# A graph layer and a routed mixture of experts on one core: first weight loads, plan words and the order of the layer products

## The reference, cut to what matters

```python
def graph(x, adj, ...):                       # 4-bit activations, 3-bit weights
    x = act_quant(layernorm(x)); w = weight_quant((w - mean) / std)
    support = act_quant(relu(x @ w))
    return (adj / s) @ support * s
def ffn(x, ...):                              # top 2 of 16 experts
    logits = x @ Wr + br
    topk_w, topk_idx = top_k(softmax(logits), 2); topk_w /= sum(topk_w)
    h = gelu(layernorm(x @ W1[e] + b1[e]) * g1[e] + be1[e])
    y = h @ W2[e] + b2[e]                     # of the two chosen experts, weighted by topk_w
x = x + graph(layernorm(x), adj, ...)
x = x + ffn(layernorm(x))
```

## Time and profile before

| | us |
|---|---|
| median of 3 runs (562.1 to 565.27) | 562.18 |
| the profiled execution | 563.38 |
| its span, first to last instruction | 561.6 |
| PE busy | 499.5 (89%) |
| DVE busy | 352.4 (63%) |
| ACT busy | 290.8 (52%) |
| POOL busy | 234.3 (42%) |

### The profile page before, as it was taken

How to read it: one execution, slowest core, us unless ns; L and a number is a source line. 1 busy time by engine, 2 the same in 40 slices (tenths; PEclk the granted TensorE clock), 3 DMA queues, 4 the chain that set the end, 5 groups by cost and what they waited for, 6 DMA issues and landing times.

```text
span 561.6 us, 10545 instructions
## 1 busy us (share of the span) xinstructions
PE 499.5 (89%) x2384; PEld 405.3 (72%) x2385; DVE 352.4 (63%) x703; ACT 290.8 (52%) x488; POOL 234.3 (42%) x303
## 2 busy tenths in 40 slices
PE   1789999999999984788999999997997999999991
PEld 1568887788777763766887788886876888778881
DVE  5797855646667584477566667666766856666440
ACT  2664644434243413326567666765866766664440
POOL 5584502321625352244344444443434454444441
PEclk9999999999999995579999999997998999999996
DMA  8522215555444528138657776778498676534442
GB/s 303 198 76 75 84 50 193 198 168 188 130 174 152 187 77 312 41 125 286 164 126 194 187 203 154 180 195 216 123 299 213 158 218 152 146 60 78 77 81 46
DMA packets 33192, 88.29 MB, mean 157 GB/s; under 512 B 6064, under 2 KB 6208, under 8 KB 33040
## 3 DMA queue, kind: packets, MB, share of 16 engines
q1 hardware_dynamic: 18912, 56.53, 30.7%
q0 software_dynamic: 9648, 23.09, 20.9%
q10 hardware_dynamic: 4608, 8.39, 3.9%
HBM read 68.60 MB, written 19.40 MB: 157 GB/s over the span
## 4 chain that ended last, share of the span: by engine, by line
PE 51%; DVE 18%; ACT 8%; issue 7%; POOL 6%; DMA 4%; DVEq 2%; ACTq 1%; SPq 1%; POOLq 0%
PE ps L1407 10%; PE ps L1406 10%; PE ps L1408 10%; PE ps L1253 5%; PE ps L1240 4%; DVE w_lo L1172 3%; PE ps L1403 3%; PE ps L1426 3%; ACT w_hi L803 2%; POOL rstd L555 2%; DMA w_raw<-in_w 2%; DVE adj_lo L922 2%; ACT adj_hi L671 2%; PE ps L1398 2%; ACT xn L700 2%
## 5 line engine op out<-in xcount | busy, mean ns | idle before, releaser
L830 ACT ACTIVATE g_sb<-ps,be_sb,g_sb 128x128 f32<-128x128 f32 x160 | 60.1, 458 | 78.9 <-PE ps L1426 78.9
L598 POOL DMA_INDIRECT xg<-xn_rows,tok_i x45 | 49.9, 1110 | 105.2 <-ACT gate L809 66.3
L1172 DVE TENSOR_TENSOR w_lo<-w_raw,w_hi x58 | 68.5, 1222 | 28.1 <-ACT w_hi L803 19.5
L1270 PE MATMUL ps<-sup,adj_hi 128*128 128x512 f32 x192 | 78.3, 408 | 2.3 <-DVE adj_lo L922 2.3
L1270 PE MATMUL ps<-sup,adj_lo 128*128 128x512 f32 x192 | 75.3, 392 | 0.0
L631 POOL DMA_INDIRECT out<-y_sb,scat_i x39 | 64.3, 1649 | 16.3 <-issue 11.7
L1408 PE MATMUL ps<-w_lo,xt_hi 128*128 (+1 forms) x168 | 68.7, 409 | 0.0
L1407 PE MATMUL ps<-w_hi,xt_lo 128*128 (+1 forms) x168 | 68.6, 408 | 0.0
L1406 PE MATMUL ps<-w_hi,xt_hi 128*128 (+1 forms) x168 | 68.6, 408 | 0.0
L922 DVE SCALAR_TENSOR_TENSOR adj_lo<-adj_raw,small,adj_hi 128x1024 fp32r<-128x1024 f32 x32 | 40.7, 1273 | 39.6 <-ACT adj_hi L671 39.5
L1407 PE MATMUL ps<-w_hi,gt_lo 128*128 (+1 forms) x160 | 63.9, 399 | 0.0
(11 more groups left out here) (172 smaller groups left out, 1001.7 us busy)
## 6 DMA issues: line engine op xcount, KB each, us to landing
w_raw<-in_w SPq DMA_DIRECT2D x64, 512.0 KB
adj_raw<-in_adj_steps SPq DMA_DIRECT2D x32, 512.0 KB, 3.5
out<-x_sb ACTq DMA_DIRECT2D x16, 256.0 KB, 3.0
xn_rows<-xn ACTq DMA_DIRECT2D x16, 256.0 KB, 2.9
x_sb<-in_x SPq DMA_DIRECT2D x3, 1024.0 KB, 12.6
gw_raw<-in_gnn_w SPq DMA_DIRECT2D x1, 1024.0 KB, 5.1
x_sb<-in_x SPq DMA_DIRECT2D x2, 512.0 KB, 7.1
xg<-xn_rows,tok_i POOLq DMA_INDIRECT x45
```

The costliest lines, as they stand in the source:

```text
L598: return pool.indirect_dma_start(xg[:, s % 2, :], None, xn_rows, bass.IndirectOffsetOnAxis(ap=tok_i[:, s:s + 1], axis=0)).then_inc(gathere ...
L830: ins = act.activation(g_sb[:, par, c * P:(c + 1) * P], ht_ps(par)[:, c * P:(c + 1) * P], ACT.Gelu, scale=g1_sb[:, bass.ds(e_s * C + c, 1) ...
L1172: ins = dve.tensor_tensor(w_lo[:, n, at], w_raw[:, n, :, :].rearrange("p a n -> p (a n)")[:, at], w_hi[:, n, at].bitcast(F32), ALU.subtract)
L1270: ins = pe.matmul(acc_bank(t), part[:, n % 2, k * P:(k + 1) * P], sup[:, first_k + k, :], start=first_k + k == 0 and part is adj_hi, stop= ...
```

## The change

SP stores the split biases in window 6 and loads the first four weight blocks (and their bias rows) in halves, one half behind each adjacency load of windows 10 to 17; the gates of all three last batches follow the windows directly. VectorE no longer makes a quarter of the first low half ahead of `find(4)`: all four quarters stand behind `sel`, ahead of the wait for the compacted table, and the low half of W1 of expert 1 stands right behind the plan, ahead of the low half of the first rows. The plan words have fields of five bits (expert and start bit together); `sel` and the columns that it is multiplied with are of the one-pass type, POOL rounds the latter (`word_r`) early in the kernel, and six one-pass products of 54 columns give three kinds of field for every slot, from which VectorE sums the words. A layer waits for the high halves, multiplies bias and the four high x high products, waits for the low half of the rows, multiplies the four low x high, waits for the low half of the weights and multiplies the four high x low.

```diff
-NO_WORD = sum((E - 1) * E ** i for i in range(5))
+FIELD = 5
+NO_WORD = sum((E - 1) << FIELD * i for i in range(5))
+BIAS_OUT_IN, WEIGHTS_IN = 6, 10
...
-    put("word_of", np.concatenate([(mine - (E - 1)) * E ** i + starts * (i < 4) * 2 ** (20 + i) for i in range(5)], 1))
-    put("begin_of", (p % PAGES == 0)[:, None] * np.array([1, 2]))
+    put("word_of", np.concatenate([mine - (E - 1) + E * starts, mine - (E - 1),
+                                   (p % PAGES == 0)[:, None] * np.ones((1, 2))], 1))
...
-            return (word >> (4 * i)) & (E - 1)
+            return (word >> (FIELD * i)) & (E - 1)
 
         def starts_in(word, i):
-            return (word >> (20 + i)) & 1
+            return (word >> (FIELD * i + 4)) & 1
...
+            def store_biases():
+
+                sp.wait_ge(bias_ok, 1)
+                for n in range(2):
+                    for h, half in enumerate((bias_hi, bias_lo)):
+                        sp.dma_start(bias_dram[n, :, h, :], half[32 * n:32 * n + E, :].bitcast(F32)).then_inc(bias_out, 16)
+
+            def first_weights(i):
+
+                n, e, h = i // 2 % 2, i // 4, i % 2
+                if not h:
+                    if e:
+                        sp.wait_ge(raw_in[n], e * 48)
+                    load_bias(n, e, slice(e * D, (e + 1) * D))
+                load_half(n, h, slice(e * P, (e + 1) * P), e)
+
             for n in range(2, STEPS + WINDOWS):
                 sp.wait_ge(adj_lo_ok, n - 1)
                 load_adj(n)
-                if n == STEPS + 14:
+                w = n - STEPS
+                if w == BIAS_OUT_IN:
+                    store_biases()
+                if w == WEIGHTS_IN:
+                    sp.wait_ge(bias_out, 64)
+                    sp.wait_ge(bias_zero, 2)
+                if WEIGHTS_IN <= w < WEIGHTS_IN + 8:
+                    first_weights(w - WEIGHTS_IN)
+                if w == 14:
                     give_gates(0)
-                if n == STEPS + 20:
+                if w == 20:
                     give_gates(1)
-            give_gates(2)
...
-            sp.wait_ge(bias_ok, 1)
-            for n in range(2):
-                for h, half in enumerate((bias_hi, bias_lo)):
-                    sp.dma_start(bias_dram[n, :, h, :], half[32 * n:32 * n + E, :].bitcast(F32)).then_inc(bias_out, 16)
-            sp.wait_ge(bias_out, 64)
-            sp.wait_ge(bias_zero, 2)
-            for n, e in ((0, 0), (1, 0), (0, 1), (1, 1)):
-                load_static(n, e)
-            give_gates(3)
-            give_gates(4)
+            for b in range(2, 5):
+                give_gates(b)
             sp.wait_ge(x_tp, 2)
             load_static(0, 2)
...
             gate_values(4)
-            split_piece(0, 0, 0, 1)
             find(4)
             val_hits(4, 0, 4)
...
             ins.then_inc(sel_ok, 1)
+            for piece in range(C):
+                split_piece(0, 0, piece, 1)
 
             dve.wait_ge(compact_mm, 1)
...
             dve.wait_ge(words_mm, 1)
-            dve.tensor_scalar(begins[:, :], words_ps[:, SLOTS // 2:SLOTS], 0.0, None, ALU.add)
-            dve.tensor_scalar(plan[:, :], words_ps[:, 0:SLOTS // 2], float(NO_WORD), None, ALU.add).then_inc(table_ok, 1)
-            for piece in range(1, C):
-                split_piece(0, 0, piece, 1)
-
+            link(dve.tensor_scalar(fields[:, :], words_ps, 0.0, None, ALU.add))
+
+            def field(kind, i):
+
+                at = kind * TAB + i
+                return fields[:, at:at + SLOTS].rearrange("p (n two) -> p n two", two=2)[:, :, 0]
+
+            dve.scalar_tensor_tensor(begins[:, :], field(2, 1), 2.0, field(2, 0), ALU.mult, ALU.add)
+            link(dve.scalar_tensor_tensor(words_f[:, :], field(1, 4), 2.0 ** FIELD, field(0, 3), ALU.mult, ALU.add))
+            for i in (2, 1, 0):
+                link(dve.scalar_tensor_tensor(words_f[:, :], words_f[:, :], 2.0 ** FIELD, field(0, i), ALU.mult, ALU.add))
+            dve.tensor_scalar(plan[:, :], words_f[:, :], float(NO_WORD), None, ALU.add).then_inc(table_ok, 1)
+            split(0, 1, 2)
...
             slot_x_lo(0, 0)
-            split(0, 1, 2)
             slot_x_lo(1, 1)
...
-            PAIRS = SLOTS // 2
-            for at, name, count in ((0, "word_of", 5), (PAIRS, "begin_of", 2)):
-                for i in range(count):
-                    for h in range(2):
-                        col = 2 * i + h if name == "word_of" else i
-                        ins = pe.matmul(words_ps[:, at:at + PAIRS], const(name)[:, col:col + 1].to_broadcast([P, P]),
-                                        sel[:, h, i:i + 2 * PAIRS].rearrange("p (n two) -> p n two", two=2)[:, :, 0],
-                                        start=i == 0 and h == 0, stop=i == count - 1 and h == 1)
+            for kind in range(3):
+                for h in range(2):
+                    col = 2 * kind + h
+                    ins = pe.matmul(words_ps[:, kind * TAB:(kind + 1) * TAB], word_r[:, col:col + 1].to_broadcast([P, P]),
+                                    sel[:, h, :], start=h == 0, stop=h == 1)
...
-            def layer(dst, n, par, e, act_hi, act_lo, done):
-
+            def layer(dst, n, s, par, e, act_hi, act_lo, lo_ok, done):
+
+                at = [bass.ds((e & 1) * (C * D) + c * D, D) for c in range(C)]
+                pe.wait_ge(split_hi[n], e + 1)
                 pe.matmul(dst, two_rows[:, :], bias_row[n][:, bass.ds((e & 3) * D, D)], start=True, stop=False)
                 for c in range(C):
-                    at = bass.ds((e & 1) * (C * D) + c * D, D)
-                    pe.matmul(dst, act_hi[:, par, c * P:(c + 1) * P], w_hi[:, n, at], start=False, stop=False)
-                    pe.matmul(dst, act_lo[:, par, c * P:(c + 1) * P], w_hi[:, n, at], start=False, stop=False)
-                    ins = pe.matmul(dst, act_hi[:, par, c * P:(c + 1) * P], w_lo[:, n, at], start=False, stop=c == C - 1)
+                    pe.matmul(dst, act_hi[:, par, c * P:(c + 1) * P], w_hi[:, n, at[c]], start=False, stop=False)
+                pe.wait_ge(lo_ok, s + 1)
+                for c in range(C):
+                    pe.matmul(dst, act_lo[:, par, c * P:(c + 1) * P], w_hi[:, n, at[c]], start=False, stop=False)
+                pe.wait_ge(split_lo[n], e + 1)
+                for c in range(C):
+                    ins = pe.matmul(dst, act_hi[:, par, c * P:(c + 1) * P], w_lo[:, n, at[c]], start=False, stop=c == C - 1)
                 ins.then_inc(done, 1)
 
             def layer_1(s, par, e):
-                pe.wait_ge(x_lo_ok, s + 1)
-                pe.wait_ge(split_lo[0], e + 1)
-                layer(h_ps(par), 0, par, e, xt_hi, xt_lo, mm1)
+                pe.wait_ge(x_hi_ok, s + 1)
+                layer(h_ps(par), 0, s, par, e, xt_hi, xt_lo, x_lo_ok, mm1)
```

47 lines of the change are left out of this document (26 added, 21 removed).

## The result

| | before | after |
|---|---|---|
| median of 4 runs each, us | 562.99 | 548.68 (548.02 to 551.03) |
| ratio, 95% interval | | 0.9747 [0.9704, 0.9790] |
| the profiled execution, us | 563.38 | 548.02 |
| its span, us | 561.6 | 546.2 |
| its mean TensorE clock | 0.949 | 0.970 |

The forecast was 546.0 for the median, in a range of 541 to 554, and 547.2 for the profiled execution. That execution took 0.8 us more; the median came out 2.7 us above, of which 0.8 is that the kernel before now has a median of 562.99 instead of 562.18.

What follows compares the result with a forecast made beforehand. Graph and expert stages were taken as TensorE-bound, with a table stage between where TensorE waits on a chain of small steps. Table -8.3 and expert -7.9 gave -16.2 us: median 562.18 to 546.0, range 541 to 554.

Steps and rivals of the forecast that it cites:

- Loads, up to the token list: Table stage, first part: earlier weight loads end ScalarE's waits, so `find(4)` begins 7.24 us earlier and the list at 224.6.
- The price of the loads: Graph stage: eight 512 KB loads behind adjacency loads on SP's queue cost 0; bounds 0 and 12.6 us.
- rival (c): Graph stage: the weight loads hold up the adjacency loads, +12.6 us, thus 558.6; chance 0.03.
- Words and first gathers: Table stage, second part: six passes free TensorE, gathers set the start; first layer product at 231.9 instead of 240.50, -8.6 us.
- Rival (b): Table stage: second gather held to 0.8 us past the end of the split beside it, +2 us, thus 548.0; chance 0.12.
- The sum: Whole kernel: -8.3 us from the table stage and -7.9 from the expert stage, together -16.2 us.
- The first one-slot expert: Expert stage, first long `w_lo` wait: new product order starts the `h_hat` transposes at 387.3 instead of 391.83, -4.5 us.
- Rival (a): Expert stage: new order gains nothing, `w_lo` waits become equally long `h_hat` waits, thus 553.9; chance 0.14.
- The second: Expert stage, second one-slot expert: `h_hat` transposes at 429.45 instead of 432.82, -3.4 us, no clock fall counted.
- Rival (d): Each of 82 layer products: TensorE's sequencer falls behind, 0.31 us each, 25 us, thus 571; chance 0.05.
- Rival (e): Table stage: shorter gaps keep the clock full, passes from 211 to 237 take half, -5 us, thus 541.0; chance 0.06.

Runs made afterwards that it cites:

- order_only: The kernel before with only the new order of the layer products; 557.71 us, ratio 0.9898.
- after_again: The kernel after, unchanged, measured and profiled a second time; 547.69 us, ratio 0.9747.
- no_loads: The kernel after with weight loads and bias stores put back behind the last window; 555.61 us, ratio 0.9866.
- no_words: The kernel after with the fourteen two-pass F32 products and four-bit fields of before; 549.18 us, ratio 0.9767.
- hold_load: The kernel after with SP's load of expert 2's W1 held until the third and fourth row blocks have landed; 548.43 us, ratio 0.9768.
- rotate_hhat: The kernel after with TensorE's slot loop turned, h_hat between the W1 split's halves, and expert 2's W1 load held for the gathers; 541.25 us, ratio 0.9612.
- plan_double: The kernel after with two more plan-word loads on TensorE's sequencer in each pair of slots; 553.55 us, ratio 0.9841.

## Why the prediction was right, point by point

**Loads, up to the token list.** Forecast 213.85 for the logits, 217.8 and 217.85 for the rank product's end and `find(4)`, 224.6 for the list; it came at 213.71, 217.46, 217.50 and 224.20. -7.64 instead of -7.24, by the same mechanism. The 0.4 us are made of 0.14 at the logits, 0.2 between them and the end of the rank products, where the clock was at 1.00 (217 to 220) instead of 0.50, and 0.05 behind. The cover for the quarter splits held: they end at 224.07, the list waits for no split.

**The price of the loads.** Taken as 0. DMA is 0.72 busy instead of 0.48 and TensorE lost nothing (48.62 of 50 us against 48.59), and ScalarE never waits for `adj_raw`, so rival (c) falls.

**Words and first gathers.** The first layer product was forecast at 231.9 and came at 231.05; 0.5 of the difference is the price for the second gather beside the split, which was not paid. Rival (b) rested on a row whose gather began 1.09 us *behind* the start of its split; here the gather began 0.13 us ahead of the split and took 0.98. That is what the row of before could have told: who began first. The prediction's own times, 227.2 for the gather and 227.6 for the split, put the gather first; so the rule that the prediction took from the Trainium skill, whole, speaks against rival (b) and not for it: by it the one that starts first goes on.

**The step that failed unseen.** The sum took the gain at the first layer product (-8.6, +0.3) for the stage's. It is lost again: the third block's gather stands behind the gate copy of the first, and its data comes 6.5 us later, so the stage's gain is the third block's, -8.02. The rows that say so were in the trace of before, where that gather is issued at 240.21 and TensorE already stood 0.21 us for its block:

```profile
240.21 0.94 POOL L598 DMA_INDIRECT xg<-xn_rows,tok_i  x1 [4.81 <-ACT gate L809]
...
246.20 0.66 PE L1398 MATMUL ps<-k_sb,xg 128*128 128x128 f32 x4 [0.21 <-DMA xg<-xn_rows,tok_i]
```

With a product that began earlier and took 4.66 us the 0.21 had to grow. That the sum came out right (-8.3 against -8.0) is luck: the first product began 0.85 us earlier than forecast and took about 1.1 us less than the 5.7 to 5.8 forecast, since the clock was back at 1.00 by 234.1, and the wait of 2.47 us that the sum did not have took all of this back. Of the 1.4 us that the sum gave the words and first gathers (8.6 at the first product less 7.24), 0.4 were left at the third block.

**The first one-slot expert.** Forecast -4.5, measured -4.40: start behind `w_hi`, a short wait for `w_lo` (0.7 forecast, 0.93), `h_hat` right behind. Rival (a) falls: the wait did not change its name.

**The second.** Forecast -3.4 at the transposes of `h_hat`, measured -2.0 there and -0.80 at the next row block. The transposes were said to start with `h_hat`, 1.35 us earlier than they did; the branch and the plan loads behind the wait weren't in the sum. Some 1.1 of the 1.2 us lost behind them are the clock, which fell at that gap (in `order_only` and `after_again`, with the same gap, it didn't, and the sum had counted no fall). This is the mis-sized term: "98% busy, so the sequencer is ahead" holds for the stretch, not behind a wait in the middle of a product, where it has nothing issued ahead. Rival (d) named that cause and put it at each of 82 products; it is real at one place, and a layer product between busy slots takes 3.10 us (368.52 to 371.62) as it took 3.11 before.

**Rival (e).** Its full clock in the table stage did not come. TensorE's clock was 0.51 from 210 to 217 and 0.52 from 220 to 234; between them it was 1.00 in this execution and 0.50 in `after_again`.

**What made up for it.** 1.61 us of clock from 265 on and 1.4 us in the first slots, neither in the sum, with 0.7 given back at the end. Thus 8.02 + 1.38 + 1.61 + 4.40 + 0.80, less 0.8 in small steps, are the 15.4 against 16.2. The two main mechanisms, the loads and the first one-slot expert, came as forecast; that the total is so near is luck, for the 2.6 us missing at the second expert and the wait for the third block are offset by gains that the sum did not have.

## What to carry to other kernels

Price a step at the last of the things that it releases, not at the first: the first product came 9.4 us earlier, and all but 8.0 us of that ended in a wait for a gather whose issue time was in the trace. An engine's sequencer that is "ahead" is so only while products are queued; behind a wait placed in the middle of a product, or right ahead of a loop's end, register loads and branches are paid in full, so put them where a whole product has been issued, and keep them few: two loads for each pass were hidden there, four were not quite. When waits for one producer are small but many, ask what stands ahead of it on its engine: moving `h_hat` between two halves of a split was worth some 4 us where the words were worth nothing that shows.

## What the runs showed of the hardware that was not expected

**Clock.** Gaps of 1.4 to 2.2 us can but need not bring TensorE down to half clock, and the longer gap is not always the one behind which it falls. Behind 2.20 us the kernel before ran at 0.60 from 265 to 269; behind 1.82 us `no_loads` ran at 0.57 from 264 to 268; behind 1.83 us the kernel after and behind 2.17 us `no_words` (256 to 260) stayed at 1.00; behind 1.45 and 1.46 us at the same instruction one execution had 1.00 and one 0.50. One microsecond of an expert's gain hung on it.

**Who starts first.** A GpSimd instruction that begins behind the start of a VectorE split beside it is held. In the kernel after POOL's `h_rs` began 0.16 us behind a split of VectorE (236.88 to 239.16) and took 2.54 us, where it takes 0.60 on average in the expert stage:

```profile
236.88 2.28 DVE L980 TENSOR_TENSOR w_lo<-w_raw,w_hi 128x2048 fp32r<-128x2048 f32 x1
237.04 2.54 POOL L647 TENSOR_TENSOR h_rs<-h_rs,k_sb 128x1 f32<-128x1 f32 x1 [3.17 <-DVE h_rs L1199]
```

while the gather that began 0.13 us ahead of its split took 0.98. The Trainium skill (SBUF — State Buffer, section "SBUF: two separate sides") says that GpSimd and a VectorE instruction with two inputs in SBUF, as the split is, share a port pair, and that whichever of the two starts first holds the pair for its whole instruction, while the other fully blocks. For GpSimd behind a split the trace agrees. The other way round it does not: the split that began 0.13 us behind the gather took 2.28 us, no more than the one in the rows above, and splits of half the size took 1.23 us behind an `h_rs` that had begun 0.53 us before them and 1.22 to 1.23 alone. Ordering the two by a tenth of a microsecond is worth up to two microseconds of GpSimd; in `hold_load` and `rotate_hhat` the first wait for `h_hat` (1.32 us) stands behind such a held `h_rs`, and an order that avoids it was not tried.

**Loads of plan words.** One costs TensorE's sequencer 0.81 us with its register work, of which 308 ns are the load itself, and the loop's branch took 221 ns. Behind the wait in the middle of a product all of it shows. Under the cover of queued products two loads for each pass cost nothing in the kernel after (a slot takes 6.92 us), and four cost about 0.2 us in most passes of `plan_double`.
